# Attention front: fp32r pairs replaced by scaled half-precision pairs

## The reference

```python
def xattn(query, key, value, w_q, w_k, w_v, w_o):       # 16 heads of 64
    q, k, v = split_heads(query @ w_q), split_heads(key @ w_k), split_heads(value @ w_v)
    scores = einsum('bhqd,bhkd->bhqk', q, k) * 64 ** -0.5
    scores = scores + (1.0 - (k_pos <= q_pos)) * -10000.0
    out = einsum('bhqk,bhkd->bhqd', softmax(scores), v)
    return merge_heads(out) @ w_o

x = x + tanh(g_xattn) * xattn(layernorm(x), ctx, ctx, w_q, w_k, w_v, w_o)
x = x + tanh(g_ffn) * ffn(layernorm(x), w_gate, w_up, w_down)   # 4-bit weights, 16-bit activations
```

## Time and profile before

| | |
|---|---|
| runs | 1375.17, 1377.19, 1378.4 us (median 1377.19) |
| profiled execution | 1376.84 us, span 1375.1 us, mean granted TensorE clock 0.968 |
| TensorE matmul busy | 1267.9 us (92%) |
| VectorE busy | 1008.5 us (73%) |
| ScalarE busy | 663.6 us (48%) |
| GpSimd busy | 238.4 us (17%) |

### The profile page before, as it was taken

One profiled execution on the slowest core, in us unless ns is written; L12 is line 12 of the kernel. 1 busy time (PEld: TensorE's weight loads), 2 busy tenths in 40 slices (PEclk: granted clock), 3 DMA queues, 4 the chain that ended last, 5 costly groups with the idle time before them and its releaser, 6 DMA issues. The chain is left out here.

```text
span 1375.1 us, 19079 instructions
## 1 busy us (share of the span) xinstructions
PE 1267.9 (92%) x6157; PEld 754.2 (55%) x6157; DVE 1008.5 (73%) x1465; ACT 663.6 (48%) x782; POOL 238.4 (17%) x331
## 2 busy tenths in 40 slices
PE   7999999999999999999999999999990069999998
PEld 6778868878887864444444444444440024444443
DVE  0379778878967666777777499989999984555544
ACT  3434443343344224444443388857768973434331
POOL 1034324314423221111111032210210000000000
PEclk9999999999999999999999999999995579999999
DMA  8002212312212338776665799963377954545453
GB/s 335 2 24 96 82 46 85 99 38 77 92 69 69 103 135 253 223 225 217 214 214 164 237 323 339 332 226 138 130 259 296 322 193 133 181 154 185 157 171 112
DMA packets 126475, 231.95 MB, mean 169 GB/s; under 512 B 38352, under 2 KB 50640, under 8 KB 126416
## 3 DMA queue, kind: packets, MB, share of 16 engines
q1 hardware_dynamic: 126128, 231.26, 49.9%
q10 hardware_dynamic: 288, 0.00, 0.0%
HBM read 136.32 MB, written 91.23 MB: 165 GB/s over the span
## 5 line engine op out<-in xcount | busy, mean ns | idle before, releaser
L1799 PE MATMUL pD<-Wh,xph 128*128 128x512 f16 x384 | 145.5, 379 | 1.0 <-DVE xpl L1774 1.0
L1276 PE MATMUL gpG<-xph,Wh 128*128 128x512 f16 x384 | 145.8, 380 | 0.2 <-DVE xpl L1198 0.2
L1276 PE MATMUL gpG<-xpl,Wh 128*128 128x512 f16 x384 | 145.8, 380 | 0.0
L1276 PE MATMUL gpG<-xph,Wl 128*128 128x512 f16 x384 | 145.8, 380 | 0.0
L1276 PE MATMUL pU<-xph,Wh 128*128 128x512 f16 x384 | 145.5, 379 | 0.0
L1276 PE MATMUL pU<-xpl,Wh 128*128 128x512 f16 x384 | 145.5, 379 | 0.0
L1276 PE MATMUL pU<-xph,Wl 128*128 128x512 f16 x384 | 145.5, 379 | 0.0
L1799 PE MATMUL pD<-Wl,xph 128*128 128x512 f16 x384 | 145.5, 379 | 0.0
L1799 PE MATMUL pD<-Wh,xpl 128*128 128x512 f16 x384 | 145.5, 379 | 0.0
L1181 ACT ACTIVATE gst<-gpG,rw 128x512 f32<-128x512 f32 x96 | 65.8, 686 | 148.1 <-PE gpG L1276 144.4
L1211 DVE TENSOR_REDUCE gmx<-gst 128x512 f32 (+1 forms) x96 | 65.5, 682 | 61.9 <-ACT gst L1181 61.7
(11 more groups left out here) (223 smaller groups left out, 2608.9 us busy)
## 6 DMA issues: line engine op xcount, KB each, us to landing
dub<-up_d SPq DMA_DIRECT2D x42, 768.0 KB, 4.8
gate_d<-gst SPq DMA_DIRECT2D x96, 256.0 KB, 2.6
gb<-gate_d SPq DMA_DIRECT2D x24, 768.0 KB, 7.1
up_d<-ust SPq DMA_DIRECT2D x72, 256.0 KB, 5.3
eu<-up_d SPq DMA_DIRECT2D x22, 768.0 KB, 6.4
xr<-xn_d SPq DMA_DIRECT2D x9, 1024.0 KB, 6.5
xin<-in_x SPq DMA_DIRECT2D x32, 256.0 KB, 2.8
x_d<-x SPq DMA_DIRECT2D x32, 256.0 KB, 2.0
```

The source lines that it names most:

```text
L1276: mm = pe.matmul(ps[:, :], Ws[:, it, kt * P:(kt + 1) * P], xs[:, kt, :], start=(kt == 0 and Ws is Wh and xs is xh), stop=(kt == KT - 1 and ...
L1799: mm = pe.matmul(pD[4 * t + q][:, :], os_[n][:, cs], Ws[:, it, :], start=(it == 0 and os_ is oh and Ws is Wh), stop=(it == IT - 1 and os_ ...
```

## The change

The pairs of A, V', x and the probabilities become fp16. fp16 has a small range of exponents, so each is multiplied by a power of two: x by 2^10, the probabilities by 2^14, both constants; for A and V' a unit is found at run time from a bound on their entries: 64 (terms of the sum) times the largest magnitude of w_q times that of k, and of w_o times that of v, and from it a unit (the two operations with 2^23 leave a power of two). Four reductions on VectorE (`largest_of`), two spreads over partitions by TensorE (`spread_bounds`, into pO) and two chains of small operations (`fit_a`, `fit_v`) do so. The units are taken back in the exponential (scale S_UNIT), in the mask (multiplied once by S_SCALE) and in the residual (O_SCALE in place of tanh(g)). The low parts, until now subtractions, become scalar_tensor_tensor (multiply, then subtract); the low part of A was one already. The number of matmuls on the tiles stays.

```diff
-                Ah = sb(early, "Ah", [P, KT, INNER], F32R)
-                Al = sb(early, "Al", [P, KT, INNER], F32R)
+                Ah = sb(early, "Ah", [P, KT, INNER], F16)
+                Al = sb(early, "Al", [P, KT, INNER], F16)
...
+X_TOP, P_TOP, M_TOP = 2.0 ** 10, 2.0 ** 14, 2.0 ** 15
...
-        xh = [sb(ph, f"xh{n}", [P, H], F32R) for n in range(2)]
-        xl = [sb(ph, f"xl{n}", [P, H], F32R) for n in range(2)]
+        xh = [sb(ph, f"xh{n}", [P, H], F16) for n in range(2)]
+        xl = [sb(ph, f"xl{n}", [P, H], F16) for n in range(2)]
...
-        pTh = sb(ph, "pTh", [P, INNER], F32R)
-        pTl = sb(ph, "pTl", [P, INNER], F32R)
+        pTh = sb(ph, "pTh", [P, INNER], F16)
+        pTl = sb(ph, "pTl", [P, INNER], F16)
...
-        Vh = sb(ph, "Vh", [P, PAIRS, H], F32R)
-        Vl = sb(ph, "Vl", [P, PAIRS, H], F32R)
+        Vh = sb(ph, "Vh", [P, PAIRS, H], F16)
+        Vl = sb(ph, "Vl", [P, PAIRS, H], F16)
...
-                        act.activation(pTh[:, cs], pT[:, cs], ACT.Copy).then_inc(pTh_done, 1)
+                        act.activation(pTh[:, cs], pT[:, cs], ACT.Copy, scale=P_TOP).then_inc(pTh_done, 1)
...
+                    if not jobs and b == 0 and ahead == 0 and n == 0:
+                        act.wait_ge(v_fit if which else a_fit, 1)
...
-                        act.activation(Ah[:, n // 2, halves[n % 2]], bank_of(k, 0, n), ACT.Copy, scale=SCALE).then_inc(ch_hi, 1)
+                        act.activation(Ah[:, n // 2, halves[n % 2]], bank_of(k, 0, n), ACT.Copy, scale=A_SCALE).then_inc(ch_hi, 1)
...
-                        act.activation(Vh[:, block_of(n), :], bank_of(k, 1, n), ACT.Copy).then_inc(ch_hi, 1)
+                        act.activation(Vh[:, block_of(n), :], bank_of(k, 1, n), ACT.Copy, scale=V_SCALE).then_inc(ch_hi, 1)
...
-                        act.activation(pr[j % 2][:, :], pr[j % 2][:, :], ACT.Exp).then_inc(exp_done, 1)
+                        act.activation(pr[j % 2][:, :], pr[j % 2][:, :], ACT.Exp, scale=S_UNIT).then_inc(exp_done, 1)
...
-                dve.scalar_tensor_tensor(out=x1[n][:, :], in0=pO[:, :], scalar=TG_X, in1=xin[j % BQ][:, :],
+                dve.scalar_tensor_tensor(out=x1[n][:, :], in0=pO[:, :], scalar=O_SCALE, in1=xin[j % BQ][:, :],
...
+            def largest_of(n, data):
+                dve.tensor_reduce(bounds[:, n:n + 1], data, X, ALU.max, apply_absolute_value=True).then_inc(bound_done, 1)
+            def fit_in(top, t, unit, inv, n, terms):
+                dve.wait_ge(bound_ps, n // 2 + 1)
+                link(dve.tensor_reduce(wide[:, n:n + 2], pO[:, 0:2 * P].rearrange("p (a k) -> p a k", a=2), X, ALU.max))
+                link(dve.tensor_scalar(top, wide[:, n:n + 1], wide[:, n + 1:n + 2], terms, ALU.mult, ALU.mult))
+                link(dve.tensor_scalar(top, top, TINY, None, ALU.max))
+                link(dve.tensor_scalar(t, top, 2.0 ** 23 + 1.0, None, ALU.mult))
+                link(dve.tensor_scalar(unit, top, -(2.0 ** 23), t, ALU.mult, ALU.add))
+                link(dve.reciprocal(inv, unit))
+            def fit_a():
+                fit_in(A_TOP, A_T, A_UNIT, A_INV, 0, HD)
+                link(dve.tensor_scalar(S_UNIT, A_UNIT, SCALE / (M_TOP * X_TOP), None, ALU.mult))
+                link(dve.tensor_scalar(S_SCALE, A_INV, M_TOP * X_TOP / SCALE, None, ALU.mult))
+                link(dve.tensor_scalar(mask[:, :], mask[:, :], S_SCALE, None, ALU.mult))
+                dve.tensor_scalar(A_SCALE, A_INV, M_TOP, None, ALU.mult).then_inc(a_fit, 1)
+                dve.wait_ge(a_fit, 1)
+            def fit_v():
+                dve.wait_ge(tanh_done, 2)
+                fit_in(V_TOP, V_T, V_UNIT, V_INV, 2, HD)
+                link(dve.tensor_scalar(V_BACK, V_UNIT, 1.0 / (M_TOP * P_TOP), None, ALU.mult))
+                link(dve.tensor_scalar(O_SCALE, TG_X, V_BACK, None, ALU.mult))
+                dve.tensor_scalar(V_SCALE, V_INV, M_TOP, None, ALU.mult).then_inc(v_fit, 1)
+                dve.wait_ge(v_fit, 1)
...
-                            dve.tensor_tensor(pTl[:, cs], pT[:, cs], pTh[:, cs].bitcast(F32), ALU.subtract).then_inc(pTl_done, 1)
+                            dve.scalar_tensor_tensor(out=pTl[:, cs], in0=pT[:, cs], scalar=P_TOP, in1=pTh[:, cs],
+                                                     op0=ALU.mult, op1=ALU.subtract).then_inc(pTl_done, 1)
...
+                if k == 0:                      # VectorE, ahead of the statistics of tile 2
+                    dve.wait_ge(v_sb, ROUNDS)
+                    largest_of(3, flat(vT))
...
+                if k == 0:                      # VectorE, behind xl of tile 1
+                    fit_v()
...
+            for r in range(2):                  # VectorE, before the steps
+                dve.wait_ge(wq_in[r], 16)
+            largest_of(0, flat(wq))
             for j in range(2):
                 statistics(0, j)
+            dve.wait_ge(k_sb, ROUNDS)
+            largest_of(1, flat(kT))
+            dve.wait_ge(id_set, 2)
+            fit_a()
+            dve.wait_ge(wo_in, 16)
+            largest_of(2, flat(wo))
...
+                if k == 0:                      # TensorE, between the keys and the first scores
+                    spread_bounds(2)
...
                 project(wv, r, wv_in, [(k_sb, 3 + r)] if r < 2 else [(v_sb, r - 1)], v_ps)
+                if r == 1:
+                    spread_bounds(0)
```

More of the change, by code:

```diff
@@ L412, in front_phase @@
         srec = sb(ph, "srec", [P, 2, HEADS], F32)
+        bounds = sb(ph, "bounds", [P, 4], F32)
+        wide = sb(ph, "wide", [P, 4], F32)
+        fit = sb(ph, "fit", [P, 16], F32)
+        (A_TOP, A_T, A_UNIT, A_INV, A_SCALE, S_UNIT, S_SCALE, V_TOP, V_T, V_UNIT, V_INV, V_SCALE, V_BACK, O_SCALE) = (
+            fit[:, n:n + 1] for n in range(14))
         pT = pb(ph, "pT", 1024)
@@ L443, in front_phase @@
         kbd_set, vb_set = sem("kbd_set"), sem("vb_set")
+        bound_done, bound_ps, fit_link, a_fit, v_fit = (sem(n) for n in ("bound", "bound_ps", "fit_link", "a_fit", "v_fit"))
         apart_p, apart_e = sem("apart_p"), sem("apart_e")
@@ L661, in high @@
                         act.wait_ge(*tile(s_ps, b, j - 2))
-                        act.activation(xh[j % 2][:, :], pX[:, :], ACT.Copy).then_inc(xh_done, 1)
+                        act.activation(xh[j % 2][:, :], pX[:, :], ACT.Copy, scale=X_TOP).then_inc(xh_done, 1)
                 def normal2():
@@ L715, in chunk_low @@
                     cs = halves[n % 2]
-                    dve.scalar_tensor_tensor(out=Al[:, n // 2, cs], in0=bank, scalar=SCALE, in1=Ah[:, n // 2, cs].bitcast(F32),
+                    dve.scalar_tensor_tensor(out=Al[:, n // 2, cs], in0=bank, scalar=A_SCALE, in1=Ah[:, n // 2, cs],
                                              op0=ALU.mult, op1=ALU.subtract).then_inc(ch_lo, 1)
@@ L719, in chunk_low @@
                     q = block_of(n)
-                    dve.tensor_tensor(Vl[:, q, :], bank, Vh[:, q, :].bitcast(F32), ALU.subtract).then_inc(ch_lo, 1)
+                    dve.scalar_tensor_tensor(out=Vl[:, q, :], in0=bank, scalar=V_SCALE, in1=Vh[:, q, :],
+                                             op0=ALU.mult, op1=ALU.subtract).then_inc(ch_lo, 1)
             def scores_down(b, j, between=lambda: None):
@@ L783, in largest, with link, flat @@
                                   apply_absolute_value=True).then_inc(x2max_done, 1)
+            seq = [0]
+            def link(ins):
+                seq[0] += 1
+                ins.then_inc(fit_link, 1)
+                dve.wait_ge(fit_link, seq[0])
+            def largest_of(n, data):
[8 more added lines that the diff above has]
+                link(dve.reciprocal(inv, unit))
+            def flat(t):
+                return t[:, :, :].rearrange("p a b -> p (a b)")
+            def fit_a():
[12 more added lines that the diff above has]
+                dve.wait_ge(v_fit, 1)
             def step(b, k, have, jobs):
@@ L858, in step @@
                     dve.wait_ge(*tile(s_ps, b, j - 2))
-                    dve.tensor_tensor(xl[j % 2][:, :], pX[:, :], xh[j % 2][:, :].bitcast(F32), ALU.subtract).then_inc(xl_done, 1)
+                    dve.scalar_tensor_tensor(out=xl[j % 2][:, :], in0=pX[:, :], scalar=X_TOP, in1=xh[j % 2][:, :],
+                                             op0=ALU.mult, op1=ALU.subtract).then_inc(xl_done, 1)
                 some(8)
@@ L960, in scores, with spread_bounds @@
                 mm.then_inc(s_ps, 1)
+            def spread_bounds(n):
+                pe.wait_ge(bound_done, n + 2)
+                for a in range(2):
+                    mm = everywhere(pe, pO[:, a * P:(a + 1) * P], bounds[:, n + a:n + a + 1], ident)
+                mm.then_inc(bound_ps, 1)
             def step(b, k, have, jobs):
```

## The result

The changed kernel takes 1366.07 us (median of four runs, 1364.05 to 1367.26) against 1376.93 us of the kernel before in the same comparison: ratio 0.9921, 95% interval 0.9906 to 0.9936. The forecast was 1366 us. The profiled execution has a span of 1363.6 us, 11.5 less.

The account below looks back on a forecast made before the run. TensorE was taken to bound the front nearly everywhere, VectorE just behind in weight-job steps. TensorE -22.1, VectorE +8.1, ScalarE +0.6 and start +2.5 sum to -10.9 us: 1366 us, range 1358 to 1371.

Parts of the forecast that it names:

- TensorE's gain: Front's values and scores matmuls: starts fall from 233.6 and 226.8 ns to 215.8, saving 22.1 us, 0.69 us a step.
- My own reason: Front matmuls: excess largest in values, where every load brings a new block, while in scores two matmuls share one.
- VectorE's share: Job steps: VectorE takes over as bound, five steps gain 0.8 us instead of 3.45; 8.1 us lost over three batches.
- Over 0.72 us: Sign of a wrong forecast: low parts on VectorE measuring over 0.72 us; their cost was taken as unchanged.
- the term for them: Last V high parts before a batch's first scores: ScalarE's column scale costs 0.1 us for each of three batches.
- ScalarE's: High parts of A and V and exponential take column scales, 686 ns against 597; 0.6 us on the path.
- The start: Four VectorE reductions, two spreads and the fit chains before the first jobs: +2.5 us, bounded below by 0.2.
- The bound of 1.5 us: Start: a slower TensorE clock behind the new wait ahead of the fifth key block would add 1.5 us.
- Sum: Whole kernel: -22.1 + 8.1 + 0.6 + 2.5 = -10.9 us, taking the profiled 1376.84 us to 1365.9, forecast 1366.
- rival (a): Job steps: VectorE isn't the bound, its pauses shrink or its work overlaps; -19.0 us, 1358 us; chance 0.12.
- (b): VectorE or start dearer: 2.6 us on three operations, clock 1.5, ScalarE unhidden 1; 1371 us; chance 0.14.
- (c): Front's TensorE pace isn't the type's: 233.6 and 226.8 ns stay, only added work remains; 1380 us; chance 0.07.

Follow-up runs that it names:

- run with the types alone: Kernel before with only the eight tiles changed from F32R to F16, no powers of two, bounds or fit: 1360.23 us (0.9887).
- exchanged loops: Kernel before, still fp32r, with the scores loop over halves moved outside the loop over the three products: 1376.34 us, one execution.
- more TensorE work: Changed kernel with pTh, pTl, Vh and Vl back in F32R, all scaling kept: 1375.02 us (0.9989).
- short links: Four semaphore increments between a weight job's small VectorE operations removed, front only: changed kernel 1361.02 us (0.9886), kernel before 1375.26 us (0.9993).
- all-three run: Changed kernel without the four job increments, vT reduced behind tile 2's statistics, normalized tile's maximum moved between the job's operations: 1354.67 us (0.9847).

## Why the prediction was right, and where its steps were off

**TensorE's gain** held: 215.9 ns against the 215.8 taken from the gate stage, 11.67 us for a step where 12.39 - 0.69 = 11.70 was said. In the last batch, with no jobs, four steps in a row took 11.67. The rule of the Trainium skill ("TensorE: Matmul & The Clock Gate", "Back-to-back issue gap"), a gap of 216 ns for 512 columns without a word of the type, agrees with f16 (215.9 ns) and not with fp32r (233.6 and 226.8). The run with the types alone has the new pace too, so it is the types that bring it. My own reason for the difference within fp32r, a new stationary block with every load in values and pairs that share one in scores, was misread (pTh stays for two matmuls in values as well) and fell with the exchanged loops. Why scores run at 227 and values at 234 ns stays open.

**VectorE's share** was the step that decided, and it came as said: residual first, beats of 13.16 us, waits for x1_done. I gave the stretch 0.8 us of gain; it was 0.96 and 1.17 in batches 1 and 2, and 1.93 in batch 0 with its longer step before. The experiments show it from both sides: less VectorE work gains 3.2 us in the stretches here and 1.6 before, more TensorE work costs 0.7 us of 2.2 in a stretch. What I had missed is why VectorE was full: in each job scale about 0.5 us were no work but a hold by GpSimd (pjs, 0.85 us in the kernel before as well). The low parts of the probabilities and of x cost nothing more (676 and 643 ns). The low parts of A and V' did: they went from 668 to 686 ns to 723 to 744 ns. "Over 0.72 us" was a sign of being wrong in the prediction, and it came for these; they lie in the start and the transitions, so the job steps, for which the sign was meant, didn't feel it. Groups by line of the changed kernel:

```profile
L852 DVE SCALAR_TENSOR_TENSOR pTl<-pT,pTh 128x512 f16<-128x512 f32 x60 | 38.1, 676 | 27.5 <-ACT pTh L638 27.5
...
L725 DVE SCALAR_TENSOR_TENSOR Al<-pT,fit,Ah 128x512 f16<-128x512 f32 x16 | 11.6, 744 | 3.7 <-ACT Ah L647 3.4
```

The two differ in the scale, a constant or a column; A's low part, which was this operation with a constant before, took 686 ns. The 743 ns of the residual, which I laid to its fp32 operand, are the column's too: with column and f16 operand it is the same 744. So ranges with a column scale are to be priced at 743, constants at 680. The scaling is why the transitions gained 5.17 us and not 6.2 (with the types alone they gained 6.8): the V' parts end later and the first residual behind them is late (the 0.49 us ahead of 194.84). So the term for them was too small: 0.1 us a transition was said, 0.5 us each is what the run with the types alone shows.

**ScalarE's** operations took what was said: 680 to 685 ns for the high parts of A and V' (686 said), 1148 ns for the exponential (1060 before).

**The start** came out as sized: from the first key block to the first pT it is 2.41 us longer, and two scores in between gained 2 x 0.26 us, so the added work costs 2.9 us, where 2.5 and 0.3 of ScalarE's were said; the run with the types alone gives 3.0. The vT reduction took 2.27 us and cost 2.2; the links of fit_a took 0.19 to 0.25 us each (0.29 behind the mask), not 0.34, which changed nothing, since fit_a and wo were covered. The bound of 1.5 us for a slower clock behind the new wait was seen in one run (short links), not in the profile of the changed kernel. The remaining 0.7 us, column scales and fit_v, weren't separated.

**Sum.** The forecast was -22.1 + 8.1 + 0.6 + 2.5 = -10.9. By the table the job steps lose 6.3 us of TensorE's gain (3 x 5 x 0.69 = 10.35, less 4.06), not 8.1, and the transitions lose 1.0, not 0.3; the start costs 2.9, as said, and 0.45 us came off ahead of the first key block. That makes -12.2 in the front, -11.5 in the span and -10.9 between the medians. The mechanisms held, but that the median hits the forecast to 0.1 us is luck in part: two terms were off by 1.8 and 0.7 us in opposite directions, and the medians are sure to some 2 us only. Of rival (a), the full gain, the all-three run shows what would have been needed for it; (b) had the cause of 0.06 us on two kinds of low parts only; (c) is refuted by the pace.

## What to carry to other kernels

When the bound engine gets faster, compare it step by step, not on average, with the next engine's unbroken chain: here 0.31 us of wait at the end of a batch's job steps before told of 8.4 us of waits in three batches after. Edits to that next engine that are worth little before such a change can be worth several times as much afterwards (1.6 against 7.5 us in the job steps), so try them again. Put work that nobody is waiting for next into a hold, and keep run-time bounds behind what the first steps need.

## What the runs showed of the hardware

A VectorE tensor_scalar of 128x16 (SBUF to SBUF) that started while a GpSimd tensor_tensor ran ended 0.03 us after it, in all twelve jobs of each of the eleven traces, and took 849 ns on average instead of 358 when it started earlier beneath it. tensor_scalar of 128x1 (154 and 214 ns), tensor_reduce (672 ns) and scalar_tensor_tensor from PSUM (743 ns) went on undisturbed beside the same operations. The Trainium skill, "Advanced Engine Details and Errata", "Mode Summary", says that GpSimd instructions and VectorE's two-port ones block each other; the runs agree in so far as one kind of VectorE operation is held and others aren't, and add that 16 columns are enough to be held and one isn't. Which mode or port an operation used no run here shows.

A column as scale cost 0.06 us on VectorE's scalar_tensor_tensor of 128x512 (A's low part, 686 to 744 and 668 to 723 ns) and 0.09 us on ScalarE (595 to 683). A dependent chain of [128, 1] operations ran at 0.19 to 0.25 us a link without, and 0.30 to 0.36 with an extra semaphore increment between wait and operation.
